# Causal convolution of a Mamba block: two of its four channel chunks as four accumulated TensorE products each, with the order of work set anew

## The chip, the cores and the metric

The kernel runs on one core of one Trainium2 chip. A core has TensorE (PE, matrix products), VectorE (DVE), ScalarE (ACT), GpSimd (POOL) and SyncE (SP, issues DMA). Each works through a queue of its own in order, and waits on semaphores that the others raise. The metric is device time in microseconds (us) of one execution; the fewer the better.

## The reference, cut to what matters

Input: 2 batches of 2048 tokens with 128 channels, all float32. Six layers in turn, each added to x:

```python
x = x + 0.5 * lora_ffn(layernorm(x))
x = x + mamba_layer(layernorm(x))
x = x + 0.5 * lora_ffn(layernorm(x))
x = x + 0.5 * moe(layernorm(x))          # 8 experts, top 2, and a shared one
x = x + linear_attention(layernorm(x))   # its context is summed over a whole batch
x = x + 0.5 * moe(layernorm(x))          # the same weights again
```

The Mamba layer, of which the change touches the second and third line:

```python
zxbcdt = u @ in_proj_w.T                 # z: 256, xBC: 512, dt: 4 channels
z, xBC, dt = split(zxbcdt)
xBC = silu(depthwise_causal_conv(xBC, conv_w, taps=4) + conv_b)
x, B, C = split(xBC)                     # 256, 128, 128
dt = softplus(dt + dt_bias); A = -exp(A_log)
# scan over tokens: h = h * exp(dt A) + dt x B^T ; y = h C
y = rmsnorm((y + D x) * silu(z)) * norm_w
out = y @ out_proj_w.T
```

## The kernel before, in words

The 4096 tokens are cut into 8 blocks of 512 (4 tiles of 128); blocks 0 to 3 are batch 0, blocks 4 to 7 batch 1. x stays in SBUF the whole time (`xs`). Each block goes through LoRA FFN, Mamba, LoRA FFN (again), gates and shared expert of the first MoE. Two blocks make a group for the experts: after both, one small product ranks the tokens (L679, in what follows "a sort"; 8 in all, 4 for each MoE; in the trace they begin at 207, 312, 465, 555, 673, 723, 805 and 876 us), GpSimd scatters the rows to DRAM sorted by expert (L1592), 12 pairs of tiles go through the experts on TensorE (L705, L723), and GpSimd gathers the results (L1618). Attention needs the whole batch's context before its output; then comes the second MoE and the store of each block.

The convolution of block b, before: TensorE projects x to each of the 4 chunks of 128 channels (L530, one product of 512 columns each). Channels lie on partitions, tokens along the row, so a tap is a shift by one column. ScalarE copies the PSUM bank to `m_pre` behind 3 columns of the block before (L1325), and writes the last tap times the same bank plus the bias to `m_cv` (L1327). VectorE adds the three other taps, one `scalar_tensor_tensor` of 128x512 each (L937), each waiting for the one before. ScalarE takes SiLU in place (L1359). GpSimd carries the 3 columns from block to block (`m_halo`, L1508 and L1516). Chunks 0 and 1 are x, 2 is B, 3 is C. Then 4 "chunks" of 128 tokens follow in sequence, each with transposes of x and B (L460), G = B C (L564), decay, and state S and output Y (L578, L588, L594), through a carried `state`.

The order of the work isn't written out by hand. Each piece (a Python generator) yields a rank, an estimated cost, and the semaphore values that it needs; `weave` merges the pieces of each engine into one queue, by the earliest time at which a stage could begin by these costs, and by rank where these are equal. The constants at the top (STEP, MAMBA_AT, ...) set the ranks. In stretches in which this planner expects TensorE to idle it puts filler products `ones x ones` of 128 columns ahead of the next stage (`keep_busy`, L455); their number (`S.filled`) also comes from the planner. PSUM has 8 banks, handed out by the planner in the same way.

A line with which several operations are recorded, such as L460 (all transposes) or L455, is a helper's. A float32 product is two records in the trace, so 826 records of L455 are 413 products. A transpose is one record.

Of the kernel before, what the change touches and what calls it, by code (L numbers as in the profile page):

```python
# [9 lines left out]
ACT = mybir.ActivationFunctionType  # L10
# [25 lines left out]

E1, IEXP, ISHARED = 8, 176, 352
# [33 lines left out]
STEP = 26.1  # L71
MAMBA_AT = 16.9
CHUNK_AT = 29.6
GAP = 6.0
FINISH_AT = 11.7
AGAIN = 3.36
GATED_AT = 17.1
SORTED_AT = 10.8
PAIR_AT = 25.3
PACE = 3.12  # L80
COMBINED_AT = 14.9
KV_AT = 73.0
# [220 lines left out]
def build(nc, d, out):  # L303

    with ExitStack() as ctx:
# [55 lines left out]
        m_xb = ring("m_xb", [P, 4, DM])  # L361
        m_xT = turned(m_xb)
# [47 lines left out]
        a_cm = ring("a_cm", [P, DM + AHEADS])  # L410
        o_qT = sb("o_qT", [P, BT])
# [32 lines left out]
        def expert_loads(e):  # L444

            return 16 * (e // 4 + 1)

        def tensor_program(e, on):
# [56 lines left out]
            def mamba(b):  # L505
# [20 lines left out]
                for c in range(XBC_CHUNKS):  # L526
                    yield T + 12.0 + 2.2 * c, 0.86, ("bank", 1), ("m_xbc", 4 * b + c), ("m_Y", 4 * b - 4), ("m_conv", 4 * b + c - 3)
                    bank = banks.take(("m_xbc", 4 * b + c))
                    on.wait_ge(*bank.freed)
                    e.matmul(bank.tile[:, :], xbc_w[:, c * P:(c + 1) * P], xT[:, :],  # L530
                             start=True, stop=True).then_inc(*S.up("m_xbc"))
                    bank.freed = ("m_tap", 4 * b + c + 1)
# [15 lines left out]
            def chunk(b, j):  # L548
# [5 lines left out]
                yield t, 1.4, ("bank", 3), ("m_gated", k + 1 - CHUNKS), ("m_cv", 4 * b + 3), ("m_cv", 4 * b + 4), ("m_seg", k + 1)  # L554
# [3 lines left out]
                on.wait_ge("m_cv", 4 * b + 3)  # L558
# [4 lines left out]
                on.wait_ge("m_cv", 4 * b + 4)  # L563
# [244 lines left out]
        def vector_program(e, on):  # L808
# [29 lines left out]
            def ffn0(i):  # L838
                T, again, b = FFN0[i]
                x, s = blk(b), i % 2  # L840
                yield T, 1.48, ("m_res", b + 1) if again else (f"x{b}", 16), ("f0_xn", i - 1)
                if again:
                    on.wait_ge("m_res", b + 1)
                else:
                    on.wait_ge(f"x{b}", 16)
# [34 lines left out]
            def mamba(b):  # L880
# [49 lines left out]
                for c in range(XBC_CHUNKS):  # L930
                    k = 4 * b + c
                    yield T + 15.0 + 2.2 * c, 2.5, ("m_conv", k), ("m_tap", k + 1), ("m_halo_in", k + 1)
                    pre = m_pre[c]
# [14 lines left out]
            def chunk(b, j):  # L948
# [14 lines left out]
                yield t + 5.0, 0.42, ("m_S", k + 1), ("m_Y", k - 1), ("m_stateq", carried(k + 1))  # L963
                on.wait_ge("m_S", k + 1)
                on.wait_ge("m_Y", k - 1)
# [212 lines left out]
            def attn_kv(b):  # L1178
# [12 lines left out]
                for j in T4:  # L1191
# [15 lines left out]
                       ("o_turn", b - BLK_PER_BATCH + 1))  # L1207
# [8 lines left out]
                on.wait_ge("o_turn", b - BLK_PER_BATCH + 1)  # L1216
                e.tensor_tensor(grouped(a_q[b % BLK_PER_BATCH][:, :, :]), grouped(qkv[:, :, 0:DM]),
# [47 lines left out]
        def scalar_program(e, on):  # L1265
# [30 lines left out]
            def mamba(b):  # L1296
# [3 lines left out]
                yield T + 3.0, 1.65, ("m_shift", b + 1), ("m_xbc", 4 * b - 4)  # L1300
                on.wait_ge("m_shift", b + 1)
                on.wait_ge("m_xbc", 4 * b - 4)
# [4 lines left out]
                yield T + 8.7, 0.78, ("w_proj", 16), ("m_turn", b + 1), ("m_out", b - 1)  # L1307
# [9 lines left out]
                for c in range(XBC_CHUNKS):  # L1317
                    k, pre = 4 * b + c, m_pre[c]
                    yield (T + 12.5 + 2.2 * c, 1.3, ("m_tap", k), ("m_xbc", k + 1), ("m_conv", k - 3), ("m_halo_out", k - 3),
# [35 lines left out]
            def conv(b, c):  # L1355
                cv, k = m_cv[b % 2], 4 * b + c
                yield MAMBA[b] + (17.5 + 2.2 * c if c < 3 else 23.0), 0.63, "silu", ("m_conv", k + 1)
# [105 lines left out]
            def decays():  # L1463
# [9 lines left out]
                  + [conv(b, c) for b in range(NBLK) for c in range(XBC_CHUNKS)]  # L1473
# [5 lines left out]
        def gpsimd_program(e, on):  # L1479
# [12 lines left out]
            def mamba(b):  # L1492
# [7 lines left out]
                for c in range(XBC_CHUNKS):  # L1500
                    k, pre = 4 * b + c, m_pre[c]
                    yield T + 11.5 + 2.2 * c, 0.19, ("m_halo_in", k), ("m_conv", k - 3), ("m_halo_out", k - 3)
                    on.wait_ge("m_conv", k - 3)
                    on.wait_ge("m_halo_out", k - 3)
                    if first:
# [145 lines left out]
            def tri_cast():  # L1651
# [5 lines left out]
            return ([tri_cast()] + [ffn0(i) for i in range(len(FFN0))] + [mamba(b) for b in range(NBLK)]  # L1657
                  + [halo(b, c) for b in range(NBLK) for c in range(XBC_CHUNKS)]
# [130 lines left out]
```

## Time and profile before

| | us |
|---|---|
| median of 3 runs | 987.66 |
| lowest, highest | 987.27, 989.98 |
| the profiled execution | 992.83 |
| its span, first to last instruction | 991.5 |

| engine | busy us | share of span |
|---|---|---|
| TensorE (PE) | 855.7 | 86% |
| VectorE (DVE) | 658.9 | 66% |
| ScalarE (ACT) | 512.4 | 52% |
| GpSimd (POOL) | 496.6 | 50% |

The busy time of TensorE holds 110.9 us of fillers (L455), and the tails of products, which overlap with the next one. The granted clock is 0.939 of full speed in the mean: most of the span at 1.00 (2.4 GHz), and some stretches at 0.50 (1.2 GHz). The table gives shares over the whole span; what bounds a stretch is read from that stretch.

### The profile page before, as it was taken

What the parts mean: (1) busy time and instruction counts of PE and PEld (TensorE: products, weight loads), DVE (VectorE), ACT (ScalarE), POOL (GpSimd) and SP (SyncE); (2) the same over time, 40 slices, a digit from 0 to 9 for tenths busy, and PEclk for the clock granted to TensorE, in tenths of its full rate; (3) what the DMA queues carried; (4) which work ended last, traced back from release to release, by engine and by line L of the source; (5) the groups of instructions that cost most, each with busy time, mean ns of one, the idle gap of its engine ahead of it and who ended that gap; (6) DMA issues with size and microseconds to landing.
All of it is one profiled execution on the core that took longest, in us unless ns stands there. A gap on an engine that the chain in (4) does not pass through costs nothing.

```text
span 991.5 us, 16555 instructions
## 1 busy us (share of the span) xinstructions
PE 855.7 (86%) x5134; PEld 664.3 (67%) x5134; DVE 658.9 (66%) x2136; ACT 512.4 (52%) x1053; POOL 496.6 (50%) x605
## 2 busy tenths in 40 slices
PE   8969799998898998699989989998899997898850
PEld 7747587877676675567766767767678766666640
DVE  4487588999898676876778756798765481462411
ACT  4865656673876675545656444553444441342310
POOL 3048553668345767432883375167345626334414
PEclk9969999999999998779999989999999999998985
DMA  9100000001010211000122022111123411412311
GB/s 304 75 1 1 0 2 1 2 15 51 6 33 27 63 49 46 27 17 21 57 73 78 30 79 82 41 38 38 57 77 89 109 44 56 123 57 72 110 51 53
DMA packets 68726, 53.44 MB, mean 54 GB/s; under 512 B 7627, under 2 KB 62923, under 8 KB 68427
## 3 DMA queue, kind: packets, MB, share of 16 engines
q1 hardware_dynamic: 60163, 34.92, 12.0%
q0 software_dynamic: 8192, 16.79, 6.0%
q8 instruction: 45, 0.74, 0.3%
q10 hardware_dynamic: 288, 0.67, 0.2%
q14 instruction: 38, 0.31, 0.1%
HBM read 26.80 MB, written 25.56 MB: 53 GB/s over the span
## 4 chain that ended last, share of the span: by engine, by line
PE 48%; POOL 14%; DVE 14%; issue 11%; DMA 6%; ACT 6%; another core or an unknown queue 0%; SPq 0%; POOLq 0%; DVEq 0%; ACTq 0%
PE psum L705 11%; PE psum L460 9%; PE psum L723 7%; POOL sorted_x L1592 5%; POOL c_y L1618 3%; DVE m_cv L937 3%; PE psum L455 3%; DMA sorted_x<-g_xn,r_slot 3%; PE psum L650 2%; PE psum L665 2%; PE psum L655 2%; PE psum L530 2%; DMA e_sx<-sorted_x 1%; DMA c_y<-sorted_y,r_slot 1%; PE psum L594 1%
## 5 line engine op out<-in xcount | busy, mean ns | idle before, releaser
L1592 POOL DMA_INDIRECT sorted_x<-g_xn,r_slot x128 | 129.8, 1014 | 119.6 <-DVE r_slot L1135 63.7
L1618 POOL DMA_INDIRECT c_y<-sorted_y,r_slot x128 | 125.1, 977 | 99.6 <-DMA sorted_y<-e_y 37.2
L705 PE MATMUL psum<-gu_w,e_sx 128*128 x368 | 135.6, 492 | 22.1 <-issue 17.0
L455 PE MATMUL psum<-ones 128*128 128x128 f32 x826 | 110.9, 285 | 8.5 <-ACT m_cv L1327 3.9
L455 PEld LDWEIGHTS psum<-ones 128*128 128x128 f32 x826 | 103.9, 200 | 16.3 <-ACT m_cv L1327 5.5
L705 PEld LDWEIGHTS psum<-gu_w,e_sx 128*128 128x128 f32 x368 | 65.7, 196 | 70.9 <-issue 52.2
L723 PEld LDWEIGHTS psum<-d_w,e_h 88*128 88x128 f32 x736 | 91.5, 193 | 16.8 <-issue 14.9
L723 PE MATMUL psum<-d_w,e_h 88*128 x736 | 99.1, 280 | 3.2 <-ACT e_h L1275 2.1
L1154 DVE TENSOR_TENSOR e_h<-e_h,psum 128x352 f32<-128x352 f32 x96 | 47.9, 503 | 78.1 <-ACT e_h L1431 55.7
L1431 ACT ACTIVATE e_h<-psum 128x352 f32<-128x352 f32 x96 | 42.9, 451 | 101.7 <-PE psum L705 82.6
L1275 ACT ACTIVATE e_h<-psum 88x512 f32<-88x512 f32 x96 | 54.2, 574 | 68.9 <-PE psum L460 64.8
L937 DVE SCALAR_TENSOR_TENSOR m_cv<-m_pre,w_proj,m_cv 128x512 f32<-128x512 f32 x96 | 78.2, 815 | 2.3
L1170 DVE SCALAR_TENSOR_TENSOR xs<-c_y,r_score,xs 128x128 f32<-128x128 f32 x128 | 39.4, 369 | 54.1 <-DMA c_y<-sorted_y,r_slot 53.4
L1158 DVE COPY e_y<-psum 128x256 f32<-128x256 f32 x96 | 38.6, 409 | 42.5 <-PE psum L723 34.9
L460 PE MATMUL psum<-w_ffn,e_h 128*88 128x128 f32 x368 | 55.4, 275 | 2.5 <-DVE e_h L1154 2.3
L1275 ACT ACTIVATE e_sx<-psum 128x256 f32<-128x256 f32 x96 | 34.3, 373 | 41.8 <-PE psum L460 30.7
L1530 POOL TENSOR_TENSOR m_seg<-w_scan,m_dt 128x512 f32<-128x512 f32 x32 | 35.0, 1098 | 38.0 <-PE psum L594 30.8
L460 PEld LDWEIGHTS psum<-w_ffn,e_h 128*88 128x88 f32 x368 | 41.7, 125 | 16.3 <-issue 9.9
L650 PE MATMUL psum<-g_xT,w_gates 128*118 128x512 f32 x96 | 50.3, 606 | 0.7 <-DVE m_ch L977 0.5
L655 PE MATMUL psum<-g_xT,w_gates 128*118 128x512 f32 x96 | 50.0, 603 | 0.0
L460 PE MATMUL psum<-w_ffn,e_sx 128*128 128x128 f32 x184 | 38.2, 306 | 12.2 <-DMA e_sx<-sorted_x 9.4
L665 PEld LDWEIGHTS psum<-w_gates,s_sg 118*128 118x128 f32 x384 | 44.8, 192 | 5.3 <-issue 2.2
(230 smaller groups left out, 1967.3 us busy)
## 6 DMA issues: line engine op xcount, KB each, us to landing
e_sx<-sorted_x SPq DMA_DIRECT2D x88, 128.0 KB
sorted_y<-e_y SPq DMA_DIRECT2D x88, 128.0 KB
xs<-in_x SPq DMA_DIRECT2D x8, 256.0 KB, 7.0
sorted_x<-c_y SPq DMA_DIRECT2D x4, 512.0 KB, 14.6
sorted_x<-g_xn,r_slot POOLq DMA_INDIRECT x128
c_y<-sorted_y,r_slot POOLq DMA_INDIRECT x128
out<-xs SPq DMA_DIRECT2D x8, 256.0 KB
gu_w<-in_gu_w SPq DMA_DIRECT2D x1, 1408.0 KB
```

The lines of the kernel that those rows point to most:

```text
L455: e.matmul(bank.tile[:, 0:P], ones[:, :], ones[:, :], start=True, stop=True)
L460: last = e.transpose(bank.tile[0:rows, j * P:(j + 1) * P], src(j), ident[:, :])
L650: e.matmul(bank.tile[0:SCW, :], sg_w[:, ch], g_xT[s][:, :], start=True, stop=True).then_inc(*S.up("s_gate"))
L655: e.matmul(bank.tile[0:SCW, :], su_w[:, ch], g_xT[s][:, :], start=True, stop=True).then_inc(*S.up("s_up"))
L665: last = e.matmul(bank.tile[:, j * P:(j + 1) * P], s_sg[s][0:SCW, c, j * P:(j + 1) * P], sd_w[0:SCW, c, :], start=(c == 0), stop=(c == SCH ...
L705: last = e.matmul(two.banks[j].tile[:, 0:2 * IEXP], e_xT[k % 4][:, j * P:(j + 1) * P], gu_w[:, bass.ds(which[j] * (2 * IEXP), 2 * IEXP)], ...
L723: last = e.matmul(bank.tile[:, j * P:(j + 1) * P], e_hT[s][0:IHALF, (2 * j + c) * P:(2 * j + c + 1) * P], d_w[:, bass.ds(which[j] * (2 * D ...
L937: v = e.scalar_tensor_tensor(cv[:, c, :], pre[:, tap:tap + BT], conv_w[:, c, tap:tap + 1], cv[:, c, :], ALU.mult, ALU.add)
L1154: e.tensor_tensor(h, h, banks.tile("e_gu", k)[:, 0:m, IEXP:2 * IEXP], ALU.mult).then_inc(*S.up("e_h"))
L1275: e.activation(dst, src, ACT.Copy).then_inc(*S.up(done))
L1592: e.indirect_dma_start(out=sorted_x[n], out_offset=bass.IndirectOffsetOnAxis(ap=r_slot[n][:, k, t:t + 1], axis=0), in_=g_xn[i % (GB + 1)][ ...
L1618: e.indirect_dma_start(out=c_y[i % 2][:, k, j, :], out_offset=None, in_=sorted_y[n], in_offset=bass.IndirectOffsetOnAxis(ap=r_slot[n][:, k ...
```

## The change

For chunks 2 and 3 (B and C) of each block, the convolution is folded into the projection: the weights of each are multiplied by each tap once at the start, and four products of 512 columns, each on the normalised input shifted by one column, accumulate in one PSUM bank. ScalarE then takes SiLU with the bias from that bank. The input is held with 3 columns of the block before it in front (`m_xh`, in place of `m_xb`). The scaled weights lie in two of the buffers `a_q` of the attention, which aren't needed until later. Chunks 0 and 1 stay as they were.

```diff
+FOLDED = [(2, 3), (2, 3)]
+TAPPED = [tuple(c for c in range(XBC_CHUNKS) if c not in folded) for folded in FOLDED]
+SCALED = tuple(sorted(set(FOLDED[0]) | set(FOLDED[1])))
-STEP = 26.1
-MAMBA_AT = 16.9
+STEP = 25.1
+MAMBA_AT = 15.9
...
+TAP_STEP = -0.46
+FOLD_AT = 29.0
...
-                for c in range(XBC_CHUNKS):
-                    yield T + 12.0 + 2.2 * c, 0.86, ("bank", 1), ("m_xbc", 4 * b + c), ("m_Y", 4 * b - 4), ("m_conv", 4 * b + c - 3)
-                    bank = banks.take(("m_xbc", 4 * b + c))
+                for n, (k, c) in enumerate(kept(b)):
+                    yield T + 12.0 + TAP_STEP * n, 0.86, ("bank", 1), ("m_xbc", k), ("m_Y", 4 * b - 4), ("m_conv", k - 3)
+                    bank = banks.take(("m_xbc", k))
...
+                for n, (k, c) in enumerate(folded(b)):
+                    yield T + FOLD_AT + 3.6 * n, 3.43, ("bank", 1), ("w_fold", len(SCALED)), ("m_fold", k), ("m_cvf", k - 1)
+                    bank = banks.take(("m_fold", k))
+                    on.wait_ge(*bank.freed)
+                    keep_busy(bank)
+                    on.wait_ge("w_fold", len(SCALED))
+                    for tap in range(DCONV):
+                        last = e.matmul(bank.tile[:, :], fold_w[c][:, tap, :], m_xh[s][:, tap:tap + BT],
+                                        start=(tap == 0), stop=(tap == DCONV - 1))
+                    last.then_inc(*S.up("m_fold"))
+                    bank.freed = ("m_cvf", k + 1)
...
-                on.wait_ge("m_Y", k - 1)
+                on.wait_ge("m_Y", k)
...
+                on.wait_ge("m_fold", FOLDED_BY[b])
+                if FOLDED[b // BLK_PER_BATCH] and b % BLK_PER_BATCH == 0:
+                    on.wait_ge("const", 3)
+                    e.activation(m_xh[s][:, 0:HALO], ones[:, 0:HALO], ACT.Copy, scale=0.0)
+                if FOLDED[b // BLK_PER_BATCH] and b % BLK_PER_BATCH < BLK_PER_BATCH - 1:
+                    e.activation(m_xh[1 - s][:, 0:HALO], banks.tile("m_x", b)[:, BT - HALO:], ACT.Identity, scale=ln_w[:, 0:1],
+                                 bias=ln_b[:, 0:1])
...
+            def folds(b, k, c):
+                cv = m_cv[b % 2]
+                yield MAMBA[b] + 17.0, 0.7, "silu", ("m_fold", k + 1), ("m_Y", 4 * b - 4)
+                on.wait_ge("m_fold", k + 1)
+                on.wait_ge("m_Y", 4 * b - 4)
+                e.activation(cv[:, c, :], banks.tile("m_fold", k)[:, :], ACT.Silu, bias=conv_b[:, c:c + 1]).then_inc(*S.up("m_cvf"))
+                yield None
...
+            def taps():
+                for c in SCALED:
+                    yield MAMBA[0] + 2.0, 1.15, ("w_proj", 16), ("w_taps", 16 * len(SCALED))
...
+                    e.tensor_tensor(fold_w[c][:, :, :], fold_w[c][:, :, :],
+                                    xbc_w[:, c * P:(c + 1) * P].unsqueeze(1).broadcast_to([P, DCONV, P]),
+                                    ALU.mult).then_inc(*S.up("w_fold"))
...
+            for n, c in enumerate(SCALED):
+                issued(256)
+                e.dma_start(fold_w[c][:, :, :], d["taps"][:, n, :, :]).then_inc(*S.up("w_taps", 16))
```

The state of the scan (`state`, L971 before, L1014 after) now waits for output Y of its own chunk, where it waited for that of the chunk before. Blocks 4 to 7 of the input share one semaphore, so the first use of any of them waits for all four loads.

The three places below show how the queues move. Names: `m_cv` is the convolved block, `m_pre` its input behind the halo, `m_xb`/`m_xh` the normalised input, `a_q` with `m_xh` the folded product, `ones` the filler, `m_dt` the step sizes.

VectorE, convolution of blocks 0 and 1, before:

```order
68 L937 SCALAR_TENSOR_TENSOR m_cv<-m_pre,w_proj,m_cv 128x512 x3
69 L908 TENSOR_SCALAR m_dt<-m_dt 128x16
70 L910 RECIPROCAL m_dt<-m_dt 128x16
71 L912 TENSOR_TENSOR m_dt<-m_dt 128x16
72 L914 TENSOR_TENSOR m_dt<-m_dt 128x16
```

and further on in the same stretch:

```order
84 L937 SCALAR_TENSOR_TENSOR m_cv<-m_pre,w_proj,m_cv 128x512 x3
85 L894 SCALAR_TENSOR_TENSOR m_ln<-m_ln 128x8
86 L895 TENSOR_SCALAR m_ln<-m_ln 128x4
87 L937 SCALAR_TENSOR_TENSOR m_cv<-m_pre,w_proj,m_cv 128x512 x3
88 L945 TENSOR_TENSOR m_dt<-m_dt,m_ex 128x16
89 L937 SCALAR_TENSOR_TENSOR m_cv<-m_pre,w_proj,m_cv 128x512 x3
90 L876 SCALAR_TENSOR_TENSOR xs<-psum,xs 128x512
91 L957 TENSOR_TENSOR m_ch<-psum,w_scan 128x128
```

The same engine and place, now:

```order
64 L972 SCALAR_TENSOR_TENSOR m_dt<-m_dt,a_exp 128x16
65 L980 SCALAR_TENSOR_TENSOR m_cv<-m_pre,w_proj,m_cv 128x512 x3
66 L945 TENSOR_TENSOR m_dt<-psum,w_scan 128x4
67 L980 SCALAR_TENSOR_TENSOR m_cv<-m_pre,w_proj,m_cv 128x512 x3
68 L945 TENSOR_TENSOR m_dt<-psum,w_scan 128x4
69 L920 SCALAR_TENSOR_TENSOR xs<-psum,xs 128x512
```

Before, 5 of the 8 triples of blocks 0 and 1 stood ahead of the first `m_ch` row; now 2 do, and block 1's two come after it.

TensorE, the same place, before:

```order
63 L455 MATMUL psum<-ones 128x128 x10
64 L541 MATMUL psum<-m_dt,w_scan 128x16
65 L542 MATMUL psum<-m_dt,w_scan 128x16
66 L543 MATMUL psum<-m_dt,ones 128x16
67 L530 MATMUL psum<-m_xb,w_proj 128x512 x3
68 L455 MATMUL psum<-ones 128x128 x5
69 L460 MATMUL psum<-w_ffn,m_xb 128x128 x4
70 L530 MATMUL psum<-m_xb,w_proj 128x512
```

and now:

```order
65 L560 MATMUL psum<-m_xh,w_proj 128x512 x2
66 L570 MATMUL psum<-m_xh,a_q 128x512 x4
67 L490 MATMUL psum<-w_ffn,m_cv 128x128 x3
68 L608 MATMUL psum<-m_cv 128x128
69 L614 MATMUL psum<-m_seg,w_scan 128x512
70 L490 MATMUL psum<-w_ffn,m_cv 128x128 x3
71 L608 MATMUL psum<-m_cv 128x128
72 L614 MATMUL psum<-m_seg,w_scan 128x512
73 L570 MATMUL psum<-m_xh,a_q 128x512 x4
```

Fillers have gone there, and folded products stand in their place, block 1's between the chunks of block 0.

TensorE, the last block (7), its step sizes (L541, now L582), before:

```order
757 L578 MATMUL psum<-m_ch 128x256
758 L541 MATMUL psum<-m_dt,w_scan 128x16
759 L542 MATMUL psum<-m_dt,w_scan 128x16
760 L543 MATMUL psum<-m_dt,ones 128x16
761 L460 MATMUL psum<-w_ffn,f_tg 128x128 x4
```

and now:

```order
664 L570 MATMUL psum<-m_xh,a_q 128x512 x4
665 L490 MATMUL psum<-w_ffn,f_xn 128x128 x4
666 L490 MATMUL psum<-w_ffn,m_cv 128x128 x3
667 L608 MATMUL psum<-m_cv 128x128
668 L614 MATMUL psum<-m_seg,w_scan 128x512
669 L511 MATMUL psum<-w_ffn,f_xn 128x136 x4
670 L622 MATMUL psum<-m_ch 128x256
671 L490 MATMUL psum<-w_ffn,e_sx 128x128 x6
672 L570 MATMUL psum<-m_xh,a_q 128x512 x4
673 L582 MATMUL psum<-m_dt,w_scan 128x16
```

The folded products of block 7 stand ahead of its step sizes. Over the whole program the queues hold 32 plain projection products before and 16 now, 64 folded ones, 413 fillers before and 235 now; 96 and 48 rows of L937; 68 and 76 table loads of ScalarE; 607 and 577 GpSimd instructions.

## Rows read from the trace of the kernel before

**Rows 1.** the profile page, busy time, and GB/s in 40 slices
```profile
PE 855.7 (86%) x5134; PEld 664.3 (67%) x5134; DVE 658.9 (66%) x2136; ACT 512.4 (52%) x1053; POOL 496.6 (50%) x605
...
PEclk9969999999999998779999989999999999998985
...
GB/s 304 75 1 1 0 2 1 2 15 51 6 33 27 63 49 46 27 17 21 57 73 78 30 79 82 41 38 38 57 77 89 109 44 56 123 57 72 110 51 53
```

**Rows 2.** busy time by stretch: PE, PEld, DVE, ACT, POOL, granted clock, DMA
```profile
0.00:207.00 207.00, 181.67 (x1130) 146.80 (x1131) 149.44 (x504) 128.64 (x272) 96.84 (x156) 0.94 0.14 46
207.00:312.00 105.00, 95.82 (x604) 76.60 (x602) 93.38 (x306) 71.53 (x157) 62.81 (x87) 0.98 0.09 26
312.00:465.00 153.00, 135.80 (x725) 101.66 (x726) 107.63 (x328) 89.33 (x185) 80.25 (x105) 0.90 0.14 39
465.00:555.00 90.00, 82.75 (x515) 65.03 (x514) 69.22 (x235) 59.14 (x113) 52.84 (x57) 0.98 0.20 58
555.00:673.00 118.00, 105.84 (x627) 80.65 (x625) 86.94 (x249) 54.57 (x99) 60.37 (x58) 0.96 0.20 57
673.00:805.00 132.00, 122.11 (x760) 95.08 (x759) 87.96 (x301) 62.22 (x133) 65.19 (x64) 0.99 0.26 73
805.00:958.00 153.00, 131.71 (x782) 98.46 (x780) 59.82 (x203) 47.01 (x100) 63.07 (x65) 0.96 0.27 77
958.00:991.00 33.00, 0.00 (x0) 0.00 (x0) 4.56 (x16) 0.00 (x0) 15.23 (x16) 0.52 0.18 50
```

**Rows 3.** the page's chain of waits, whole span: by engine, then by line
```profile
PE 48%; POOL 14%; DVE 14%; issue 11%; DMA 6%; ACT 6%; another core or an unknown queue 0%; SPq 0%; POOLq 0%; DVEq 0%; ACTq 0%
PE psum L705 11%; PE psum L460 9%; PE psum L723 7%; POOL sorted_x L1592 5%; POOL c_y L1618 3%; DVE m_cv L937 3%; PE psum L455 3%; DMA sorted_x<-g_xn,r_slot 3%; PE psum L650 2%; PE psum L665 2%; PE psum L655 2%; PE psum L530 2%; DMA e_sx<-sorted_x 1%; DMA c_y<-sorted_y,r_slot 1%; PE psum L594 1%
```

**Rows 4.** the chain by line, in 0 to 207, then in 385 to 430
```profile
by line: DVE m_cv L937 12.6%; issue 11.3%; ACT f_xn L1270 4.4%; PE psum L530 3.0%; PE psum L460 2.6%; DMA xs<-in_x 2.6%; POOL m_ch L1538 2.6%; DVE m_dt L921 2.3%; POOL m_g L1548 2.3%; ACT m_xb L1304 2.3%; POOL m_ch L1535 2.3%; POOL m_seg L1
...
by line: PE psum L530 9.6%; PE psum L594 9.6%; DVE m_dt L918 8.9%; PE psum L460 8.5%; PE psum L455 6.0%; DVE m_cv L937 5.1%; PE psum L588 4.8%; PE psum L499 4.6%; issue 4.6%; PE psum L723 4.0%; PE psum L570 3.8%; PE psum L500 3.8%; PE psum 
```

**Rows 5.** groups of operations, one form each; busy us, mean ns
```profile
L937 DVE SCALAR_TENSOR_TENSOR m_cv<-m_pre,w_proj,m_cv 128x512 f32<-128x512 f32 x96 | 78.2, 815 | 2.3
L455 PE MATMUL psum<-ones 128*128 128x128 f32 x826 | 110.9, 285 | 8.5 <-ACT m_cv L1327 3.9 <-POOL ones L1643 1.9 <-DVE xs L1078 1.2
L530 PE MATMUL psum<-m_xb,w_proj 128*128 128x512 f32 x64 | 35.0, 638 | 2.5 <-ACT m_cv L1327 2.2 <-DVE f_tg L870 0.3
L1327 ACT ACTIVATE m_cv<-psum,w_proj 128x512 f32<-128x512 f32 x32 | 25.2, 788 | 0.0
L1325 ACT ACTIVATE m_pre<-psum 128x512 f32<-128x512 f32 x32 | 19.4, 605 | 9.7 <-PE psum L530 6.0 <-DVE m_cv L937 2.4 <-issue 1.0
L1431 ACT ACT_TABLE_LOAD x15 | 19.2, 1283 | 0.3
L1530 POOL TENSOR_TENSOR m_seg<-w_scan,m_dt 128x512 f32<-128x512 f32 x32 | 35.0, 1098 | 38.0 <-PE psum L594 30.8
```

**Rows 6.** TensorE in order of time, a 512-column product, a Y; all Y products
```profile
153.11 1.02 PE L655 MATMUL psum<-g_xT,w_gates 128*118 128x512 f32 x2
153.97 0.60 PE L523 MATMUL psum<-w_proj,m_xb 128*128 128x260 f32 x2
...
78.17 0.59 PE L588 MATMUL psum<-state,m_cv 128*128 128x256 f32 x2
79.44 0.50 PE L460 MATMUL psum<-w_ffn,m_cv 128*128 128x128 f32 x3
...
L594 PE MATMUL psum<-m_ch,m_seg x256: 218/275/421, 76.8 to 491.1; 128*128 128x64 f32 x128
```

**Rows 7.** busy time in two short stretches of convolution; columns as in rows 2
```profile
52.00:64.00 12.00, 4.43 (x13) 2.51 (x12) 11.27 (x36) 7.13 (x13) 3.37 (x7) 0.62 0.00 0
402.00:420.00 18.00, 10.72 (x42) 8.46 (x42) 17.10 (x30) 8.30 (x13) 6.73 (x10) 0.72 0.08 23
```

**Rows 8.** TensorE in order of time, the step sizes of block 7
```profile
412.01 0.61 PE L541 MATMUL psum<-m_dt,w_scan 128*128 128x16 f32 x2 [5.43 <-DVE f_tg L870]
```

More of the change, by code:

```diff
@@ L410, in build @@
         a_cm = ring("a_cm", [P, DM + AHEADS])
+        fold_w = {c: a_q[n] for n, c in enumerate(SCALED)}
         o_qT = sb("o_qT", [P, BT])
@@ L446, in expert_loads, with x_loads, kept, left @@
             return 16 * (e // 4 + 1)
+        def x_loads(b):
+            return 16 if b < 4 else 16 * (NBLK - 4)
+        def kept(b):
+            return list(enumerate(TAPPED[b // BLK_PER_BATCH], TAPPED_BY[b]))
+        def left(b, n):
+            return 0 if b % BLK_PER_BATCH == 0 else TAPPED_BY[b - 1] + n + 1
+        def folded(b):
+            return list(enumerate(FOLDED[b // BLK_PER_BATCH], FOLDED_BY[b]))
         def tensor_program(e, on):
@@ L929, in mamba @@
                                        ALU.mult, ALU.mult).then_inc(*S.up("m_dta"))
[L930 to L933, printed above, removed]
+                for n, (k, c) in enumerate(kept(b)):
+                    yield T + 15.0 + TAP_STEP * n, 2.5, ("m_conv", k), ("m_tap", k + 1), ("m_halo_in", k + 1)
+                    pre = m_pre[k % 4]
                     on.wait_ge("m_tap", k + 1)
@@ L1316, in mamba @@
                     e.activation(g[:, j, :], banks.tile("m_z", 4 * b + j)[:, 0:DINNER], ACT.Silu).then_inc(*S.up("m_silu_z"))
[L1317 to L1319 removed]
+                for n, (k, c) in enumerate(kept(b)):
+                    pre = m_pre[k % 4]
+                    yield (T + 12.5 + TAP_STEP * n, 1.3, ("m_tap", k), ("m_xbc", k + 1), ("m_conv", k - 3), ("m_halo_out", k - 3),
                            ("m_Y", 4 * b - 4))
@@ L1472, in scalar_program @@
                   + [residual(b) for b in range(NBLK)] + [softplus(b) for b in range(NBLK)]
-                  + [conv(b, c) for b in range(NBLK) for c in range(XBC_CHUNKS)]
+                  + [conv(b, n, k, c) for b in range(NBLK) for n, (k, c) in enumerate(kept(b))]
+                  + [folds(b, k, c) for b in range(NBLK) for k, c in folded(b)]
                   + [chunk(b, j) for b in range(NBLK) for j in T4] + [finish(b) for b in range(NBLK)]
@@ L1499, in mamba @@
                 e.tensor_tensor(rstd, veps, neghalf[:, :].unsqueeze(1).broadcast_to([P, 2, 4]), ALU.pow).then_inc(*S.up("m_rstd"))
-                for c in range(XBC_CHUNKS):
-                    k, pre = 4 * b + c, m_pre[c]
-                    yield T + 11.5 + 2.2 * c, 0.19, ("m_halo_in", k), ("m_conv", k - 3), ("m_halo_out", k - 3)
+                for n, (k, c) in enumerate(kept(b)):
+                    pre = m_pre[k % 4]
+                    yield T + 11.5 + TAP_STEP * n, 0.19, ("m_halo_in", k), ("m_conv", k - 3), ("m_halo_out", k - 3), ("m_halo_out", left(b, n))
                     on.wait_ge("m_conv", k - 3)
                     on.wait_ge("m_halo_out", k - 3)
+                    on.wait_ge("m_halo_out", left(b, n))
                     if first:
@@ L1763 @@
             i["L0_attn_conv_b"].reshape(XBC_CHUNKS, P).T, i["L0_attn_ln_w"], i["L0_attn_ln_b"]),
+        "taps": every_row(i["L0_attn_conv_w"].reshape(XBC_CHUNKS, P, DCONV)[list(SCALED)].transpose(0, 2, 1)).reshape(
+            P, len(SCALED), DCONV, P),
         "w_scan": side_by_side(
```

74 lines of the change are left out of this document (42 added, 32 removed).

## The prediction, made before the changed kernel was run

> **What bounds the kernel now.** I read the busy shares first, then busy time by stretch, then the chain of waits, then the groups of the operations that are touched. TensorE is busy 86% of the span and VectorE 66% [rows 1]. That makes TensorE look like the bound, but the figure has two kinds of air in it. 110.9 us are fillers [rows 5], and a record's duration is longer than its pitch: a product of 512 columns holds its engine for 153.97 - 153.11 = 0.86 us, and its two records have 638 ns each in the mean [rows 5, 6]. If I price TensorE's queue at the pitch (0.86 us for 512 columns, others by their columns, a transpose half), it holds 641 us of real work and 88 us of fillers, 729 us for a span of 991.5. So no engine is full. The time is made of hand-overs between engines that are each about three quarters full. The chain of waits says so too: PE 48%, POOL 14%, DVE 14%, issue 11% [rows 3].
>
> The stretches of [rows 2] end where the first to fifth and the seventh sort begin. In 207 to 312 VectorE is busy 93.38 of 105 us, its fullest stretch; in 0 to 207 it's 149.44. In 0 to 207 the largest line on the chain is VectorE's convolution (L937) with 12.6%, which is 26.1 us; in 385 to 430 it has 5.1%, 2.3 us [rows 4]. Together that is 28.4 us, which fits the 3% of the page [rows 3]. In both places the granted clock is low while VectorE works on taps: 0.62 in 52 to 64 and 0.72 in 402 to 420, a mix of the levels of 1.2 and 2.4 GHz, after stretches in which TensorE stood idle, with TensorE busy 4.43 of 12 us in the first, and VectorE 11.27 of 12 and 17.10 of 18 [rows 7]. At block 7 TensorE stands idle 5.43 us ahead of the step sizes (L541), until VectorE is through with what they need [rows 8]. After 491.1 no scan of a Mamba block is left [rows 6]. From there experts, attention, scatters and gathers set the pace, and from 958 on only gathers and the last additions, with TensorE at 0.00 [rows 2].
>
> **What goes.** VectorE: 48 of the 96 tap instructions at 815 ns [rows 5], 39.1 us busy. ScalarE: 16 copies at 605 ns and 16 scalings at 788 ns, 22.3 us; a SiLU from the bank takes the place of one in place. GpSimd: 30 instructions fewer, nearly all small halo copies, hidden. TensorE: 178 of 413 fillers, whose pitch is 0.213 us each (88 us over 413): 38 us.
>
> **What comes.** TensorE: 64 folded products for 16 plain ones, 48 x 0.86 = 41.3 us. Fillers and products nearly cancel, and the queue's sum goes from 729 to 732 us. ScalarE: 8 more table loads (68 to 76) at 1283 ns [rows 5], +10.3 us, and 8 tiny copies of 3 columns. ScalarE still has 10 us less, and it's on the chain for 6% [rows 3], so I count -1 for it.
>
> The Trainium skill speaks against this part: "ScalarE: Activation LUTs", section "What ACT_TABLE_LOAD costs", gives about 2.66 us for each switch, a load of 1283 ns and a drain of about as much. The load agrees with the trace; the drain doesn't show in the 15 loads of the row, which had 0.3 us idle ahead in all. By the page ScalarE's balance would be 21.3 us more instead of 10.3, about even with what it loses. That would take away my -1 and nothing else.
>
> **On the path, term by term.**
> (1) Taps. Half of the chain's 28.4 us goes: -14.2. At least 0, if other lines take their place, and at most the 39.1 us.
> (2) Products. What decides is not the sum but whether more stands ahead of each landmark. With the same prices, TensorE's queue up to the output product of blocks 0 to 7 holds 66, 99, 143, 185, 229, 285, 340, 373 us before and 64, 99, 140, 177, 221, 283, 321, 382 now. VectorE's queue up to the residual of the same blocks, priced by the mean of each group, holds 71, 111, 159, 207, 258, 308, 371, 406 and now 57, 97, 137, 180, 221, 274, 310, 368. So the folded products go mostly into room that fillers had, and each block finishes behind the same TensorE work and 14 to 61 us less VectorE work. To the end the queue is 3 us longer; at the 74% (729/991.5) at which it's used, +4. Bounds: -12.8, if only the fillers' part of the chain falls (3% of 991.5 is 29.7 us, times 178/413 is -12.8) and products are hidden; and +16.9, if products stand on the chain as often as L530 does now (2% of 991.5 is 19.8 us for 32 x 0.86 = 27.5, so 0.72 x 41.3 = 29.7, less 12.8).
> (3) Clock. In 52 to 64 and around 402 to 420 TensorE gets products where it had none. At full clock its 4.43 and 10.72 us [rows 7] would take less: -2, between -6 and 0.
> (4) State waits for its own Y. Y (L588 and L594) takes 79.44 - 78.17 = 1.27 us [rows 6]. Behind the waiting addition stand the next tokens' VectorE rows, and state_q on GpSimd. Chunks follow each other every 13 us (32 of them from 76.8 to 491.1 [rows 6]), so most are covered: +2, between 0 and 32 x 1.27 = 41.
> (5) Start. Scaling the weights is two GpSimd instructions of 128x512; the nearest row is 1098 ns [rows 5]. They stand ahead of the third layernorm's power, in the first microseconds, when the chain is on ScalarE (L1270) and the loads of x [rows 4]. Two DMAs of 256 KB more delay what is loaded behind them by 512 KB at 304 GB/s [rows 1], 1.7 us; the GB/s are 1 from the third slice on, so nothing waits later. The common semaphore of blocks 4 to 7 costs nothing for that reason. 0, at most +4.
> (6) Ranks. All later work is reordered. Up to the fifth sort TensorE's queue holds 506 us before and 507 now, VectorE's 542 and 491. I take 0; the uncertainty is that of the forecast below.
> Sum: -14.2 + 4 - 2 + 2 + 0 - 1 = -11. The profiled execution of 992.83 becomes 982; it lies 5.2 above the median of 987.66, so the forecast is **976**.
>
> A check by stretches. TensorE's queue in the seven stretches (the last two rows as one) goes 149, 83, 109, 71, 94, 110, 112 to 156, 105, 92, 70, 84, 115, 110; VectorE's 166, 98, 111, 75, 93, 98, 66 to 157, 101, 85, 68, 80, 107, 67. If each stretch scales with TensorE's content alone, the span becomes 994, +3. If it scales with the sum of both, it becomes 963, -28. The term sum lies between.
>
> **Rivals.**
> A, both count alike: each stretch scales with both engines' content, -28, so 960. For it: VectorE has the fullest stretch [rows 2] and the taps lead the chain early. Against: PE has 48% of the chain, and after 555 nothing of the 39 us is left to save unless earlier finishes carry through scatters and gathers.
> B, products on the chain (the slower side): in 207 to 312 TensorE's queue grows from 83 to 105 us, where it was busy 95.82 of 105 [rows 2]. The second sort then comes late, the experts of group 1 with it, and later stretches don't give it back. Price: the product term at its bound of +16.9 instead of +4, and taps of which only half the credit is kept (-7), since after the first stretch VectorE then waits for TensorE; with (3) to (6) as above, -1: +9. 1002 for the profile, 997 in the median. It decides if the second sort starts later than 330 and the fourth later than 560. For it: the rows of PE. Against: the fillers went as the products came, and the content at each block's end is even.
> C, no change: blocks finish earlier, but batch 1's attention and the last groups wait for GpSimd and DMA as before; 985 to 991.
> That the fold doesn't happen is excluded by the queue: 64 folded products and 48 taps stand in it.
>
> **Numbers.** A measurement of this kernel tells about 0.3%, 3 us, from no change. Chances: forecast 0.44 (966 to 984), A 0.18, C 0.15, B 0.23. So faster 0.62, same 0.15, slower 0.23. The range takes in most of A and B: 957 to 998; the forecast's own is 966 to 984.
>
> **What would show it.** Right: L937 at 48 and about 39 us, with chain share in 0 to 207 at half of 12.6%; the first Y some 8 us earlier than 76.8; clock above 0.9 in what was 52 to 64; the last Y before 482 (now 491.1); the fourth sort before 550. Wrong: a folded product's line among the first three of the chain in 207 to 465, TensorE waiting for a bank or for SiLU (`m_cvf`) ahead of the chunk's transposes, VectorE idle behind the state's wait for over 10 us in all, or a second sort later than 330.

## The result, and the profile after

The changed kernel took 963.61 us in the median (963.0 to 965.38) against 988.78 on the same chip: ratio 0.9749, 95% interval 0.9727 to 0.9771, 25 us faster. I forecast 976 within 957 to 998. Sign and range held; of the gain I had seen somewhat less than half (11 us of 25).

The page of the changed kernel: busy time, clock, the chain by engine, then by line.

```profile
PE 840.1 (87%) x4874; PEld 633.9 (66%) x4874; DVE 617.5 (64%) x2088; ACT 506.9 (53%) x1037; POOL 487.0 (51%) x575
...
PEclk9999999999899999999999989988999998998985
...
PE 42%; POOL 20%; issue 12%; DVE 12%; DMA 10%; ACT 3%; SPq 0%; POOLq 0%; DVEq 0%; ACTq 0%
POOL sorted_x L1654 8%; PE psum L749 8%; PE psum L490 6%; POOL c_y L1680 6%; PE psum L767 5%; DMA sorted_x<-g_xn,r_slot 4%; PE psum L570 3%; DMA c_y<-sorted_y,r_slot 3%; DMA e_sx<-sorted_x 2%; PE psum L694 2%; PE psum L699 2%; PE psum L709 2%; DVE xs L1213 2%; PE psum L638 1%; POOL m_seg L1592 1%
```

Against [rows 3], the convolution of VectorE is gone from the list, and the folded product (L570) stands in it with 3%. The share of PE fell from 48% to 42%, that of POOL rose from 14% to 20% and that of DMA from 6% to 10%.

The same kernel's groups that answer to [rows 5], and then the chain by line in its first 198 us:

```profile
L980 DVE SCALAR_TENSOR_TENSOR m_cv<-m_pre,w_proj,m_cv 128x512 f32<-128x512 f32 x48 | 43.1, 898 | 1.1
L570 PE MATMUL psum<-m_xh,a_q 128*128 128x512 f32 x128 | 59.9, 611 | 0.1
L485 PE MATMUL psum<-ones 128*128 128x128 f32 x470 | 62.8, 283 | 3.8 <-POOL ones L1705 1.9 <-ACT m_g L1448 1.9
L1413 ACT ACTIVATE m_cv<-psum,w_proj 128x512 f32<-128x512 f32 x16 | 10.9, 683 | 8.5 <-PE psum L570 8.4
```

```profile
by line: issue 10.3%; PE psum L570 8.7%; PE psum L490 5.5%; PE psum L560 3.8%; PE psum L529 3.6%; ACT f_xn L1315 3.3%; PE psum L530 3.2%; PE psum L614 3.0%; PE psum L638 3.0%; DMA xs<-in_x 3.0%; POOL m_seg L1592 2.9%; PE psum L553 2.9%; ACT
```

Where VectorE's taps had 12.6% of the chain [rows 4], none of the lines named here is a tap. Over the whole chain the kept taps still have 0.6% of the span, 6 us. The folded product is the first line after issue, 8.7% of 198 us, 17 us. So work went from one engine's place on the chain to another's, and yet all came earlier. The kept taps are also slower, 898 ns in the mean for 815 [rows 5], so VectorE's time in taps fell by 78.2 - 43.1 = 35.1 us and not by 39.1; why they are slower was not tested.

Busy time by stretch, in the columns of [rows 2], cut at this kernel's own first five sorts, and near its end:

```profile
0.00:198.00 198.00, 179.61 (x1018) 135.79 (x1019) 145.56 (x521) 134.19 (x288) 103.27 (x157) 0.98 0.16 51
198.00:322.00 124.00, 118.71 (x649) 86.19 (x648) 90.15 (x322) 83.10 (x170) 60.40 (x77) 0.97 0.09 28
322.00:434.00 112.00, 105.17 (x614) 79.09 (x613) 80.23 (x274) 73.51 (x151) 75.49 (x95) 0.98 0.15 47
434.00:518.00 84.00, 77.66 (x479) 59.25 (x477) 62.31 (x207) 50.01 (x96) 43.37 (x46) 1.00 0.20 63
518.00:622.00 104.00, 94.13 (x575) 72.28 (x574) 73.27 (x219) 51.06 (x100) 47.63 (x46) 0.97 0.20 58
930.00:962.00 32.00, 0.00 (x0) 0.00 (x0) 4.57 (x16) 0.00 (x0) 15.23 (x16) 0.50 0.17 49
```

The second stretch is longer than before (124 us for 105), the third much shorter (112 for 153). In the stretch in which VectorE was fullest before (93.38 of 105 us), it is busy 90.15 of 124 now. The tail after the last expert is as it was.

And TensorE at the two places of [rows 7] and [rows 8]: the start of the scan, and block 7's step sizes.

```profile
50.79 1.88 PE L560 MATMUL psum<-m_xh,w_proj 128*128 128x512 f32 x4
52.51 3.60 PE L570 MATMUL psum<-m_xh,a_q 128*128 128x512 f32 x8
55.95 0.49 PE L490 MATMUL psum<-w_ffn,m_cv 128*128 128x128 f32 x3
...
368.78 3.70 PE L570 MATMUL psum<-m_xh,a_q 128*128 128x512 f32 x8
372.32 0.29 PE L582 MATMUL psum<-m_dt,w_scan 128*128 128x16 f32 x2
```

```profile
46.00:58.00 12.00, 12.00 (x62) 8.11 (x61) 11.55 (x42) 9.47 (x18) 6.27 (x8) 1.00 0.00 0
362.00:380.00 18.00, 15.06 (x68) 9.18 (x68) 14.50 (x31) 11.62 (x21) 15.21 (x19) 1.00 0.24 69
```

The first stretch is filled with products, no idle time stands ahead of L582, and the granted clock of both is 1.00, 2.4 GHz throughout. The four products of 512 columns take 55.95 - 52.51 = 3.44 us, 0.86 each.

The starts of the sorts (the last column: the end of the span), in us, from the traces of the two kernels and of the experiments told below (Y is the output product of a scan, S its state product, "old" a constant of the kernel before):

| kernel | 1 | 2 | 3 | 4 | 5 | 6 | 7 | 8 | end |
|---|---|---|---|---|---|---|---|---|---|
| before | 207 | 312 | 465 | 555 | 673 | 723 | 805 | 876 | 991.5 |
| changed | 198 | 322 | 434 | 518 | 622 | 692 | 776 | 843 | 961.7 |
| before, new ranks | 222 | 365 | 513 | 595 | 733 | 797 | 872 | 946 | 1066.6 |
| changed, old ranks | 193 | 312 | 451 | 556 | 665 | 726 | 808 | 879 | 995.7 |
| changed, old ranks of first half | 185 | 303 | 448 | 552 | 652 | 733 | 816 | 887 | 1004.8 |
| changed, old ranks of second half | 201 | 324 | 434 | 521 | 640 | 703 | 788 | 863 | 982.8 |
| changed, old GATED_AT | 193 | 312 | 439 | 527 | 663 | 712 | 807 | 874 | 990.7 |
| before, thin taps | 206 | 313 | 462 | 552 | 669 | 721 | 805 | 879 | 996.6 |
| changed, double taps | 223 | 356 | 471 | 557 | 661 | 730 | 814 | 882 | 999.8 |
| changed, thin fold | 202 | 323 | 433 | 518 | 622 | 691 | 776 | 844 | 960.8 |
| changed, three folded | 200 | 328 | 450 | 540 | 657 | 710 | 797 | 866 | 982.9 |
| changed, no fillers | 207 | 329 | 439 | 524 | 629 | 699 | 783 | 850 | 964.8 |

The two kernels before without fillers (experiments 7 and 8) are left out: their profiled executions took over 1% longer than their medians. Between before and changed, 30 us are won at the third sort, 51 at the fifth, 31 at the sixth, 33 at the eighth and 30 at the end.

### The profile page after: what moved, and what is told of

Same layout as the page of the kernel before. It is cut to its first block, busy times and chain, and to the rows that moved or that the text cites. A ratio compares the mean times of both kernels' runs of the same rounds, so it can differ in the third digit from the quotient of the medians.

```text
span 961.7 us, 15892 instructions
## 1 busy us (share of the span) xinstructions
PE 840.1 (87%) x4874; PEld 633.9 (66%) x4874; DVE 617.5 (64%) x2088; ACT 506.9 (53%) x1037; POOL 487.0 (51%) x575
## 4 chain that ended last, share of the span: by engine, by line
PE 42%; POOL 20%; issue 12%; DVE 12%; DMA 10%; ACT 3%; SPq 0%; POOLq 0%; DVEq 0%; ACTq 0%
POOL sorted_x L1654 8%; PE psum L749 8%; PE psum L490 6%; POOL c_y L1680 6%; PE psum L767 5%; DMA sorted_x<-g_xn,r_slot 4%; PE psum L570 3%; DMA c_y<-sorted_y,r_slot 3%; DMA e_sx<-sorted_x 2%; PE psum L694 2%; PE psum L699 2%; PE psum L709 2%; DVE xs L1213 2%; PE psum L638 1%; POOL m_seg L1592 1%
## 5 line engine op out<-in xcount | busy, mean ns | idle before, releaser
L1680 POOL DMA_INDIRECT c_y<-sorted_y,r_slot x128 | 125.6, 981 | 99.8 <-DMA sorted_y<-e_y 38.9
L485 PE MATMUL psum<-ones 128*128 128x128 f32 x470 | 62.8, 283 | 3.8 <-POOL ones L1705 1.9
L485 PEld LDWEIGHTS psum<-ones 128*128 128x128 f32 x470 | 59.2, 199 | 6.7 <-issue 2.1
L1201 DVE COPY e_y<-psum 128x256 f32<-128x256 f32 x96 | 39.1, 409 | 33.1 <-PE psum L767 32.4
L570 PE MATMUL psum<-m_xh,a_q 128*128 128x512 f32 x128 | 59.9, 611 | 0.1
L709 PE MATMUL psum<-w_gates,s_sg 118*128 118x128 f32 x384 | 45.6, 276 | 1.0 <-DVE s_sg L1115 0.9
```

Source lines behind the costliest of these rows:

```text
L485: e.matmul(bank.tile[:, 0:P], ones[:, :], ones[:, :], start=True, stop=True)
L570: last = e.matmul(bank.tile[:, :], fold_w[c][:, tap, :], m_xh[s][:, tap:tap + BT], start=(tap == 0), stop=(tap == DCONV - 1))
L709: last = e.matmul(bank.tile[:, j * P:(j + 1) * P], s_sg[s][0:SCW, c, j * P:(j + 1) * P], sd_w[0:SCW, c, :], start=(c == 0), stop=(c == SCH ...
L1680: e.indirect_dma_start(out=c_y[i % 2][:, k, j, :], out_offset=None, in_=sorted_y[n], in_offset=bass.IndirectOffsetOnAxis(ap=r_slot[n][:, k ...
```

## The experiments

Each ratio is to the kernel before on the same chip, with its 95% interval; the changed kernel stands at 0.9749. "Fold" is the folded products alone, "ranks" the constants that set the order.

**1. The ranks without the fold.** The kernel before with

```diff
-STEP = 26.1
-MAMBA_AT = 16.9
+STEP = 25.1
+MAMBA_AT = 15.9
...
-GATED_AT = 17.1
+GATED_AT = 25.1
```

and likewise all others.

> The kernel before with the changed kernel's rank constants and nothing else. Theory F (the fold pays: work moved from VectorE to TensorE): without the fold these ranks are not worth anything, ratio to before 1.00 to 1.02. Theory R (the ranks pay, the fold is a wash): most of the 25 us is here, ratio below 0.985.

Measured: 1069.55 us, ratio 1.0771 [1.0709, 1.0833]. The ranks don't pay by themselves, far from it. My upper end of 1.02 was much too low.

**2. The fold without the ranks.** The changed kernel with the constants of before (and `TAP_STEP = 2.2`).

> The changed kernel with the rank constants of before (the spacing of the two kept taps 2.2, the folded products' rank offset 29.0 as in the changed kernel). Theory F: the fold alone gives at least 12 of the 25 us, ratio 0.97 to 0.988. Theory R: ratio 0.995 or above.

Measured: 1000.51 us, 1.0073 [1.0042, 1.0104]. That is in the range of theory R for this run, but theory R fell with the run before, and theory F falls here: in this order the fold alone makes the kernel 0.7% slower. Its first sort is 14 us earlier than before, and by the fourth nothing is left of it. Neither part pays by itself; the pair gives 25 us. So neither theory holds. The folded products need ranks of their own, which the kernel before doesn't have (`FOLD_AT` stays at 29.0), so this is one old order for them and not the only one.

**3. VectorE relieved in the old order.** The kernel before with

```diff
+                        w = BT if c < 2 else 4
-                        v = e.scalar_tensor_tensor(cv[:, c, :], pre[:, tap:tap + BT], conv_w[:, c, tap:tap + 1], cv[:, c, :],
+                        v = e.scalar_tensor_tensor(cv[:, c, 0:w], pre[:, tap:tap + w], conv_w[:, c, tap:tap + 1], cv[:, c, 0:w],
```

> The kernel before, every queue the same, but the three VectorE taps of channel chunks 2 and 3 done on 4 of 512 columns: that part of the convolution is left out. VectorE loses some 33 us of work, TensorE gains none. It bounds what the relief of VectorE alone is worth. Theory F: 15 to 30 us faster, ratio 0.970 to 0.985, most of it before the fourth sort. If taps were covered by other work, under 5 us.

Measured: 993.53 us, 0.9996 [0.9962, 1.0031]; VectorE's busy time fell from 658.9 to 633.3 us. 25.6 us less on the engine that had 28.4 us of taps on the chain, and no gain at all. Its chain in the first 207 us shows what took the place:

```profile
by line: PE psum L455 9.4%; issue 9.2%; DVE m_cv L938 5.7%; ACT f_xn L1271 4.4%; PE psum L460 4.0%; PE psum L530 3.0%; PE psum L594 2.9%; DMA xs<-in_x 2.8%; PE psum L499 2.5%; DVE m_dt L921 2.3%; PE psum L570 2.2%; POOL m_g L1549 2.2%; PE p
```

The taps fell from 12.6% to 5.7%, and the fillers (L455), which no line named in [rows 4] for this stretch is, lead with 9.4%. The chain of waits ahead of the first output product (start, us, what) shows one such place, and under it TensorE in order of time at the same place in the kernel before:

```profile
71.99 1.09 PE psum L570 x2
73.08 3.57 PE psum L455 x32
76.65 0.43 PE psum L578 x2
77.09 0.84 PE psum L594 x8
...
72.84 3.73 PE L455 MATMUL psum<-ones 128*128 128x128 f32 x32
76.41 0.60 PE L578 MATMUL psum<-m_ch 128*128 128x256 f32 x2
```

The same 32 records of fillers stand there before; then the chain ran through VectorE and GpSimd beside them, and now it runs through the fillers: L455 has 59.5% of it in 72 to 78. The first Y starts at 76.9 as before (76.8 in [rows 6]).

**4. TensorE relieved in the new order.** The changed kernel with

```diff
+                        w = BT if tap == 0 else 16
-                        last = e.matmul(bank.tile[:, :], fold_w[c][:, tap, :], m_xh[s][:, tap:tap + BT],
+                        last = e.matmul(bank.tile[:, 0:w], fold_w[c][:, tap, :], m_xh[s][:, tap:tap + w],
```

> The changed kernel, every queue the same, but three of the four products of each folded chunk done on 16 of 512 columns: those taps are left out. TensorE loses 48 products, 0.82 us each, 39 us at full clock. It prices what the folded products cost on the path. My term (2) said 4 us net; if they are hidden in waits 0 to 5 us faster than the changed kernel (ratio to before 0.970 to 0.975); if they stand on the chain as often as the trace has them (3% of the span), 15 to 30 us faster (0.945 to 0.96). A lower granted clock in their place could eat part of it.

Measured: 962.3 us, 0.9682 [0.9633, 0.9731]. 0.7 points under the changed kernel: some 7 us for 39 us of products, with intervals that just touch. It lies between what I gave for products hidden in waits (0.970 to 0.975) and for products that stand on the chain (0.945 to 0.96), close to the first. Its sorts are the changed kernel's, within some 4 us. Busy time and clock of its first two stretches:

```profile
0.00:198.00 198.00, 173.26 (x995) 139.03 (x996) 141.86 (x513) 129.71 (x279) 100.80 (x153) 0.91 0.16 51
198.00:322.00 124.00, 114.72 (x670) 89.86 (x669) 92.45 (x328) 86.66 (x179) 61.23 (x81) 0.93 0.09 27
```

The granted clock is 0.91 and 0.93, where the changed kernel has 0.98 and 0.97. What this lower clock costs, and so how much of the relief it takes back, no run separates.

**5 and 6. Which half of the ranks.** The changed kernel with the second half's constants of before:

```diff
-KV_AT = 74.7
-SECOND_AT = [173.0, 212.0, 217.0, 272.0, 351.0, 328.0, 502.0, 451.0]
-GATED_AGAIN_AT = 41.6
+KV_AT = 73.0
+SECOND_AT = [189.0, 216.0, 233.0, 282.0, 336.0, 338.0, 462.0, 452.0]
+GATED_AGAIN_AT = 40.9
```

> The changed kernel with the second half's rank constants (KV_AT, SECOND_AT, GATED_AGAIN_AT) of before. If the gain is made in the first half and carried through (Theory H1), the sorts up to the third stay where they are in the changed kernel and the whole is at most 8 us slower than it (ratio to before 0.975 to 0.983). If the second half's ranks made it (H2), 0.985 to 1.00.

and with all others of before instead (STEP to PAIR_AT; `TAP_STEP` and `FOLD_AT` stay):

> The changed kernel with the first half's rank constants (STEP to COMBINED_AT) of before, and the second half's of the changed kernel. H1: this loses nearly all of the gain, ratio 0.995 to 1.01. H2: ratio 0.975 to 0.985.

Measured: 982.18 us, 0.9875 [0.982, 0.993], and 1010.61 us, 1.0185 [1.0125, 1.0245]. The first keeps its first four sorts within 3 us of the changed kernel's and loses 18 us at the fifth, 21 at the end; so half of the gain (12.5 us of 25) rests on the ranks of the second half. The ratio lies in the range that I gave for H2, above that of H1, while the early sorts stayed as H1 had it. The second ratio is above H1's range of 0.995 to 1.01, and far above H2's. That kernel has the earliest first sort of all (185) and still ends behind the kernel before: an early start of one group says nothing of the end, and without the first half's ranks nothing of the gain is left. The two halves don't add up: the second half's new ranks are worth 12.5 us behind the new first half, and behind the old one the kernel with them (1.0185) is slower than with old ranks throughout (1.0073).

**7 and 8. Fillers and relief in the old order.** Both without fillers, the second with the thin taps of experiment 3 as well.

```diff
-                for _ in range(int(S.filled - FILLED * late / FILLER)):
+                for _ in range(0):
```

> The kernel before with all 413 fillers left out, queues otherwise the same. Where fillers stand on the chain (3% of the span) this saves, where they hold the clock up it costs: granted clock below 0.90, and a time 0 to 3% above before.

> As the run before it, and the taps of channel chunks 2 and 3 on 4 of 512 columns as in the run of thin taps (that part of the convolution is left out). In the run of thin taps 32 filler records of 3.57 us stood on the chain ahead of the first output product, in place of the taps. Theory Q (fillers, planned for the old waits, ate the relief): against the run without fillers this is 8 us faster or more. Theory O (the relief is off the path whatever the fillers, since the queues' order binds): less than 3 us between the two.

Measured: 1000.19 us, 1.0087 [1.0055, 1.0119], as expected, and 988.72 us, 0.9941 [0.9907, 0.9974]. Between the two 11.5 us. So in the old order VectorE's relief is worth 1.5 points without fillers and nothing with them. That is what theory Q said (8 us or more), and it takes the fillers' part as far as 11.5 of the 25.6 us.

**9. VectorE's work given back in the new order.** The changed kernel with, for each kept chunk,

```diff
+                    for tap in range(HALO):
+                        own(e.scalar_tensor_tensor(spare[:, :], pre[:, tap:tap + BT], conv_w[:, c, tap:tap + 1],
+                                                   spare[:, :] if tap else pre[:, 0:BT], ALU.mult, ALU.add))
+                        settled()
```

> The changed kernel, every queue the same, with three extra tap instructions of 128x512 on a spare tile (results unused) ahead of the three of each kept chunk: VectorE has the 39 us back that the fold took away, TensorE keeps the fold. The counterpart of the thin taps in the kernel before. Theory S (VectorE's relief is spent: the new order relies on it): 12 to 30 us slower than the changed kernel, ratio to before 0.985 to 1.005. Theory O (VectorE's relief is off the path): under 4 us slower, ratio below 0.98.

Measured: 999.65 us, 1.0057 [1.0024, 1.009], 3.1 points or 31 us above the changed kernel, just above the range of theory S. VectorE's busy time rose by 34.9 us (617.5 to 652.4). The extra work stands on the chain of the whole span in its own right, and the kept taps with it:

```profile
by line: issue 11.2%; PE psum L750 8.6%; POOL sorted_x L1659 8.0%; PE psum L491 6.9%; PE psum L768 5.3%; POOL c_y L1685 4.4%; DVE spare L981 3.5%; DMA sorted_x<-g_xn,r_slot 3.4%; DVE m_cv L985 2.6%; DMA c_y<-sorted_y,r_slot 2.6%; DMA e_sx<-
```

3.5% and 2.6% of 999.8 us are 61 us together, where the taps had some 6 us of the changed kernel's chain. The loss is made by the third sort (471 for 434) and kept. So VectorE work of this size is worth nothing in the old order with its fillers (25.6 us taken away) and all of the gain in the new one (34.9 us put back). The two runs aren't mirror images: the work put back stands ahead of the kept taps and not where the folded-away taps stood, and no run adds the same work to the old order.

**10. Fillers in the new order.** As in experiment 7.

> The changed kernel without its 235 fillers, queues otherwise the same. In the kernel before 413 fillers were worth 0.9%. With folded products in the places of fillers the clock should depend less on the rest: 0.92 or more, and a time 0 to 0.6% above the changed kernel (ratio to before 0.974 to 0.981). If fillers hold it up as before, 0.9% or more above.

Measured: 968.94 us, 0.9755 [0.9718, 0.9792]. As expected: the changed kernel has no measurable use of its 235 fillers, where the kernel before was 0.9% slower without its 413. The mean clock is 0.930 without them (0.952 with).

**11. One rank of before.**

```diff
-GATED_AT = 25.1
+GATED_AT = 17.1
```

> The changed kernel with one rank constant of before: GATED_AT 17.1 in place of 25.1, by which the gates and shared expert of a block stand 8 us lower in rank against the Mamba work of later blocks. If holding them back for the scans is what makes the second to fourth sort early, this loses a third of the gain or more: ratio to before above 0.983, and the third sort later than 442 (434 in the changed kernel, 465 before). Otherwise 0.975 to 0.980.

Measured: 992.79 us, 0.9991 [0.9967, 1.0014]. One constant takes all of the gain. But not where I expected it: the third sort stays at 439. Then the last Y comes at 476.4 for 458.7, and the fifth sort at 663 for 622:

```profile
L638 PE MATMUL psum<-m_ch,m_seg x256: 219/275/422, 62.9 to 476.4; 128*128 128x64 f32 x128
```

One thing that changed its place can be read from the traces. These are the gathers of expert results (L1680, 64 in the first MoE) that begin ahead of the fifth sort, first in the changed kernel, then here, and the chain here between the fourth sort and the fifth:

```profile
L1680 POOL DMA_INDIRECT c_y<-sorted_y,r_slot x51: 940/957/1267, 363.8 to 621.8; - x51
...
L1680 POOL DMA_INDIRECT c_y<-sorted_y,r_slot x64: 939/947/1853, 362.5 to 641.9; - x64
...
by line: POOL c_y L1680 18.8%; DMA c_y<-sorted_y,r_slot 14.6%; issue 14.4%; POOL sorted_x L1654 9.6%; DMA sorted_x<-g_xn,r_slot 4.9%; PE psum L490 3.9%; PE psum L767 3.8%; PE psum L749 3.7%; DVE xs L1213 3.6%; DMA sorted_y<-e_y 2.8%; PE psu
```

With 25.1, 13 of the 64 gathers come after the fifth sort; with 17.1 all 64 come before it, and gathers and their transfers have a third of the chain in that stretch (in the changed kernel L1680 has 2.8% of 518 to 622). In the kernel before 62 come before it, with the old second half (experiment 5) 62 as well. This is a reading and not a test, and it isn't the whole: with all old ranks (experiment 2) 54 come before it, and the fifth sort is as late (665). The constant moves everything that is reckoned from it (sort, pairs, gathers, keys and values), so the run says that this offset decides, not through which of them. The mean granted clock is 0.952, that of the changed kernel, so the gain is not a matter of the mean clock.

**12. Three chunks folded.** `FOLDED = [(1, 2, 3), (1, 2, 3)]`.

> The changed kernel with three of four channel chunks folded (1, 2, 3), ranks as in the changed kernel. VectorE loses 20 us more, TensorE gets 20 us more. If VectorE's relief still pays more than the products cost: ratio to before below 0.972. If TensorE is now the fuller engine, or the ranks don't fit: 0.98 to 1.01, which I hold likelier.

Measured: 982.62 us, 0.9875 [0.9832, 0.9917]. 13 us slower than with two, in the upper case as I held likelier; whether by TensorE's load or by ranks that don't fit, this run can't tell. No run has a lower ratio than the changed kernel but experiment 4, which leaves work out.

## Why the prediction was right, and by half

**The check by stretches** was the better half of the prediction. Scaling each stretch with the priced queues of both engines gives 206, 120, 123, 85, 104, 141, 185 us. Measured: 198, 124, 112, 84, 104, 154, 186. Its sum of -28 was my rival A; -30 on the profiled execution is what came. That the sums agree so well is in part luck, since single stretches are off by -8, -11 and +13 us and these errors cancel. What I held against A, that earlier finishes wouldn't carry through scatters and gathers, did not come true here: of the 30 us at the third sort all are there at the end. But they don't carry by themselves. With the old second half (experiment 5) the third sort is as early and 21 us are lost behind it.

**Term (6), the ranks at 0, is the step that failed.** I summed the fold's terms to -11 in an order that I took as given. Fixed in the old order the fold measures +7 (experiment 2), and setting the order anew for it is worth 3.2 points, 32 us (1.0073 to 0.9749). So two errors, 18 us too good for the fold by itself and 32 us too little for the ranks, partly cancel in the sum of -11: that sign and range held is to this extent luck. The queue totals that I quoted under (6), 542 to 491 us of VectorE ahead of the fifth sort, could have been a warning: 51 us less ahead of a landmark, when only 39 were removed, means that other work has also moved behind it, as 11 of GpSimd's gathers did (62 of 64 began ahead of it before, 51 now). That the fifth sort came just 51 us earlier proves nothing; the queues of the other engines had changed too.

**Term (1), taps, -14.2.** On the chain the taps fell from 28.4 us to about 6, where I had counted on half. Whether that is worth anything depends on the order: 0 in the old one with its fillers (experiment 3), 11.5 without them (7 and 8), 31 in the new one (9). A line's share of the chain, halved, predicted none of the three.

**Term (2), products, +4, bounds -12.8 to +16.9.** Experiment 4 has 7 us, between 0 and 14 by the intervals, which the value taken fits. It prices the products alone; what taking out the 178 fillers gave, which the term nets against them, no run isolates. The products' share of the chain (3% of 961.7 is 29 us) was as high as in my upper case, but a share isn't a price: with the products thinned, busy time and clock changed and the end came only 7 us earlier.

**Term (3), clock, -2.** Both low stretches went to 1.00. No run isolates it; experiments 2 and 11, with the same mean of 0.952 and no gain, show that the mean clock isn't the cause.

**Term (4), the state's wait, +2.** I misread it, here and in the description of the change. The value k of `m_Y` is reached when the chunk before is through, which is the last reader of that buffer, and not the chunk's own Y. The kernel before waited for the Y of one chunk earlier still. So the wait is tighter by one chunk, and the reason for the +2, a chunk's own Y, is not there. The trace agrees: none of its 30 additions is released by a Y.

```profile
L1014 DVE TENSOR_TENSOR state<-state_q,psum x30: 405/414/423, 70.3 to 458.1; 128x256 f32<-128x256 f32 x30
its engine sat idle before it (us, times) until:
  PE psum L622: 7.9, 9
  POOL state_q L1605: 1.3, 2
```

L622 is S, POOL is the state's decay. The term shows as 0.

**Term (5) and ScalarE.** No row of the start stands out. ScalarE's busy time fell by 5.5 us (512.4 to 506.9) where I had counted 10, and its chain share fell from 6% to 3%. Neither was tested by itself.

**Rival B** was half there. The second sort came at 322, 10 us later than before though not after 330, and L570 has 10.1% of the chain in 198 to 322, the second share after issue. But the next stretch gave all of it back, and the fourth sort at 518 is far from 560. **Rival C**, no change, is excluded by the interval. The marks for right were met: L937's 48 instructions (at 43.1 us instead of 39), first Y at 63.2 (some 8 us earlier than 76.8 expected, 13.6 measured), clock, last Y at 458.7, fourth sort at 518. The mark for wrong on the chain was not met: over the whole of 207 to 465 L570 has 4.9%, behind issue and four other lines.

What stays open: through which pieces GATED_AT does its work (the gathers are only a reading), what share of the 32 us other orders could have given with one constant of the old ranks changed, what the same extra work on VectorE would cost in the old order, and why the relief without fillers (11.5) is still far from 31.

## What to carry to other kernels

A queue written for the old balance can hide the worth of a relief. Before an engine is called covered, thin its work out with the queues fixed and take the fillers out too; then do the reverse in the new order. Price work that is moved by what each engine's queue holds ahead of each landmark, not by halves of chain shares, and never set an order that was made anew at 0: here the change was worth nothing without it. A rank table belongs to one structure; on the other it cost 7.7%.

## What the runs showed that I had not expected

A relief of VectorE that is worth 11.5 us without fillers was worth nothing with them, and the chain shows fillers where the waits used to be, while having these fillers was worth 0.9% in all. And the granted clock fell from 0.98 to 0.91 in the first stretch when three of four folded products were thinned. That useful products now do the fillers' work would fit this, and would fit that the changed kernel loses nothing measurable without its 235 fillers (its mean clock then is 0.930); no run tests it by itself.
